# Four output products moved ahead of the last turn, two copies given to ScalarE, and some stages of head and end at other steps

## What is computed

```python
x = x + xattn(layernorm(x), ctx)     # 6 layers: self attention, cross attention over
                                     # 2048 context rows, feed-forward; all have a null key
x = x + attn(layernorm(x))           # one causal attention, 16 heads of 8
x = x + ffn(layernorm(x))            # a recurrent cell over the 4 elements:
#   f = sigmoid(x_t @ wf.T + c @ uf.T + bf); i = sigmoid(...); g = tanh(...)
#   c = f * c + i * g
#   out_t = tanh(x_t @ wo.T + c_final @ uo.T + bo)      for each element t
```

## Time and profile before

| | |
|---|---|
| median of 3 runs | 2582.73 us (2582.8, 2582.73, 2577.71) |
| the profiled execution | 2579.03 us |
| its span, first to last instruction | 2577.3 us |
| PE, DVE, ACT, POOL busy | 96%, 86%, 80%, 24% |
| granted TensorE clock, mean | 0.979 of full |
| head, before the heart of the first run | 0 to about 85 us |
| end, after the last heart | from about 2489 us |

### The profile page before, as it was taken

The page is one execution under the profiler, slowest core; times in us unless marked ns, Lnnn a source line. Parts: engine busy times, 40 slices in busy tenths (PEclk is TensorE's granted clock), DMA queues, the critical chain, the costliest instruction groups (busy, mean ns, idle before and its releaser), DMA issues.

```text
span 2577.3 us, 38071 instructions
## 1 busy us (share of the span) xinstructions
PE 2483.9 (96%) x12652; PEld 1532.9 (59%) x12652; DVE 2220.7 (86%) x4417; ACT 2053.5 (80%) x3977; POOL 615.2 (24%) x400
## 2 busy tenths in 40 slices
PE   4899999999999999999999999999999999999987
PEld 2456656656656656566566566566566566665566
DVE  6789889898898898898898898988988988989865
ACT  2788888888888888878888888888888888888743
POOL 3322312312313213123123123122132131231000
PEclk8899999999999999999999999999999999999986
DMA  3000010000001001001001001001001000000000
GB/s 130 25 9 17 26 36 17 25 11 37 26 14 39 15 11 47 9 17 53 9 17 47 9 17 53 9 17 47 3 23 36 17 25 30 17 9 26 1 1 5
DMA packets 16573, 63.56 MB, mean 25 GB/s; under 512 B 2241, under 2 KB 7410, under 8 KB 11642
## 3 DMA queue, kind: packets, MB, share of 16 engines
q1 hardware_dynamic: 16378, 61.13, 7.3%
HBM read 48.25 MB, written 0.29 MB: 19 GB/s over the span
## 4 chain that ended last, share of the span: by engine, by line
PE 71%; DVE 17%; ACT 5%; issue 4%; POOL 2%; DMA 0%; SPq 0%; DVEq 0%; POOLq 0%; ACTq 0%
PE psS L1108 20%; PE psO L1156 11%; PE psO L1157 11%; PE psO L1159 11%; DVE PL L690 5%; PE psL L1202 3%; ACT P L940 2%; PE psL L1213 2%; PE psL L1108 2%; PE psL L1220 2%; ACT PH L937 2%; DVE back_x L762 1%; DVE V L740 1%; POOL back_rstd L455 1%; PE psL L1101 1%
## 5 line engine op out<-in xcount | busy, mean ns | idle before, releaser
L937 ACT ACTIVATE PH<-psS 128x512 fp32r<-128x512 f32 x1536 | 1031.9, 672 | 180.7 <-PE psS L1108 160.9
L940 ACT ACTIVATE P<-psS 128x512 f32<-128x512 f32 x1536 | 1038.0, 676 | 109.8 <-DVE PL L690 109.7
L690 DVE TENSOR_TENSOR PL<-P,PH 128x512 fp32r<-128x512 f32 x1536 | 1040.5, 716 | 81.1 <-ACT P L940 71.3
L1108 PE MATMUL psS<-QT,KT 128*128 128x512 f16 x3072 | 923.6, 384 | 0.4 <-ACT P L940 0.3
L1156 PE MATMUL psO<-PH,V 128*128 128x512 f32 x1536 | 876.7, 571 | 0.0
L1157 PE MATMUL psO<-PH,VL 128*64 128x512 f32 x1536 | 607.1, 395 | 0.0
L1159 PE MATMUL psO<-PL,V 128*128 128x512 f32 x1536 | 606.0, 395 | 0.4 <-DVE PL L690 0.4
L1108 PEld LDWEIGHTS psS<-QT,KT 128*128 128x128 f16 x3072 | 218.1, 100 | 367.7 <-issue 282.4
L1156 PEld LDWEIGHTS psO<-PH,V 128*128 128x128 f32 x1536 | 292.4, 190 | 177.8 <-ACT PH L937 9.8
L1159 PEld LDWEIGHTS psO<-PL,V 128*128 128x128 f32 x1536 | 288.4, 188 | 152.4 <-DVE PL L690 0.9
L455 POOL TENSOR_TENSOR rn<-ssc,neghalf 128x16 f32<-128x16 f32 (+4 forms) x75 | 240.8, 3211 | 341.1 <-DVE ssc L624 264.1
(11 more groups left out here) (370 smaller groups left out, 2858.4 us busy)
## 6 DMA issues: line engine op xcount, KB each, us to landing
ctx_sb<-ctxT SPq DMA_DIRECT2D x24, 1024.0 KB, 4.7
KT<-KT SPq DMA_DIRECT2D x48, 256.0 KB, 3.7
W<-wpack SPq DMA_DIRECT2D x6, 1280.0 KB, 5.3
W<-wpack SPq DMA_DIRECT2D x6, 1088.0 KB, 7.4
W<-wpack SPq DMA_DIRECT2D x6, 576.0 KB, 5.7
KT<-biasM SPq DMA_DIRECT2D x1, 1024.0 KB
W<-tail_w SPq DMA_DIRECT2D x1, 832.0 KB
P<-biasW SPq DMA_DIRECT2D x1, 512.0 KB
```

What stands on the lines that cost most here:

```text
L690: nc_v.tensor_tensor(PL[:, here, :], P[:, t % PSLOTS, :], PH[:, here, :], ALU.subtract).then_inc(sem("p_lo"), 1)
L937: nc_a.activation(PH[:, t % HSLOTS, :], bank, ACT.Exp, scale=SIM_SCALE).then_inc(sem("p_hi"), 1)
L940: nc_a.activation(P[:, t % PSLOTS, :], bank, ACT.Exp, scale=SIM_SCALE).then_inc(sem("ca_exp"), 1)
L1108: ins = mm(bank, keys[part], q, start=(part == 0), stop=(part == 1))
```

## The change

The output products of each element become stages (`v_output0` to `v_output3`). Three stand ahead of `v_turn_z`, the fourth behind `v_gates3`. In setup, ScalarE makes the copy of the null values and scales them in place; VectorE waits for it and does the third operation. ScalarE has only that stage ahead of its first work of the head. One semaphore is folded into another, with the same order. The tables have some stages at other steps.

```diff
-            140: ["v_turn_z"],
-            141: ["v_gates3"],
+            140: ["v_output0", "v_output1", "v_output2", "v_turn_z"],
+            141: ["v_gates3", "v_output3"],
...
             def s_values():
-                setup(nc_v.tensor_copy(NVH[:], NV))
-                setup(nc_v.tensor_scalar(NV, NV, row_whole, None, ALU.mult))
+                dve.wait_ge(sem("values"), 1)
                 setup(nc_v.scalar_tensor_tensor(out=NVH[:], in0=NVH[:].bitcast(F32), scalar=row_high, in1=NV, op0=ALU.mult, op1=ALU.add))
...
+            def s_values():                              # ScalarE, first in its order
+                act.wait_ge(sem("consts_in"), 16 * 6)
+                nc_a.activation(NVH[:], NV, ACT.Copy)
+                nc_a.activation(NV, NV, ACT.Copy, scale=row_whole).then_inc(sem("values"), 1)
...
+                def output():
+                    pe.wait_ge(sem("z_T"), b + 1)
+                    mm(BANKS_OUT[b][:, 0:128], zT[:, b, :], tail_w(T_WO), start=True, stop=False)
+                    mm(BANKS_OUT[b][:, 0:128], ones[:], bo_row[:], start=False, stop=False)
...
-            for t in range(B):
-                mm(BANKS_OUT[t][:, 0:128], zT[:, t, :], tail_w(T_WO), start=True, stop=False)
-                mm(BANKS_OUT[t][:, 0:128], ones[:], bo_row[:], start=False, stop=False)
             pe.wait_ge(sem("c_ready"), B + 1)
```

More of the change, by code:

```diff
@@ L261, in build @@
             12: ["f_kv2", "h_kv2"], 13: ["f_kv3", "h_kv3"], 14: ["b_wo", "t0_turn_y2"],
-            18: ["f_turn_q_sa", "h_turn_q_sa", "b_turn", "t0_qkv"],
-            20: ["f_turn_k_sa", "h_turn_k_sa", "b_gate", "f_sn", "h_sn", "t1_turn_fin"], 21: ["t0_s0"],
+            18: ["f_turn_q_sa", "b_turn", "t0_qkv"], 19: ["h_turn_q_sa"],
+            20: ["f_turn_k_sa", "b_gate", "f_sn", "t1_turn_fin"], 21: ["h_turn_k_sa", "h_sn", "t0_s0"],
             22: ["f_sk0", "h_sk0", "t1_proj"], 23: ["f_sk1", "h_sk1", "t0_s1"], 25: ["f_sv0", "h_sv0", "t1_turn_y2"],
[4 rows of a table removed]
@@ L269, in build @@
[L269 to L272, removed]
[6 rows of a table removed]
[5 rows of a table added]
+            52: ["f_turn_ca", "h_turn_ca", "l_gate"], 53: ["t0_turn_z", "t1_pv1", "f_proj_ca", "h_proj_ca"],
@@ L279, in build @@
+            54: ["u_turn_fin"], 55: ["t1_pv2", "f_turn_k", "h_turn_k"], 56: ["u_proj"], 57: ["t1_pv3"], 58: ["l_up"],
+            59: ["t1_turn_o"], 60: ["t1_wo"], 61: ["h_turn_q_ca", "l_down"], 63: ["f_turn_q_ca", "t1_turn_z"],
+            64: ["b_down"], 68: ["u_turn_y2", "u_qkv"], 70: ["v_turn_fin"], 72: ["u_gates0"], 73: ["v_proj"], 75: ["u_s0"],
[6 rows of a table added]
         }
         PLAN_ACT = {
-            2: ["f_raw_sa", "h_raw_sa"], 3: ["f_raw_sa2", "h_raw_sa2"], 8: ["f_sq_sa", "h_sq_sa", "f_kraw0", "h_kraw0"],
@@ L282, in build @@
-            9: ["f_kraw1", "h_kraw1"], 10: ["s_table"], 12: ["h_hi_sa", "f_kraw2", "h_kraw2"], 13: ["f_hi_sa"],
-            15: ["f_kraw3", "h_kraw3"], 16: ["f_ksq", "h_ksq"], 17: ["f_QT_sa", "h_QT_sa"], 20: ["f_sne", "h_sne"],
[3 rows of a table removed]
-            47: ["t1_back2"], 53: ["f_raw_ca", "h_raw_ca", "f_sq_ca", "h_sq_ca"], 54: ["l_tanh"], 55: ["f_KT", "h_KT"],
-            57: ["h_hi_ca"], 59: ["f_hi_ca"], 61: ["h_QT_ca"], 63: ["f_QT_ca"], 72: ["u_gates0"], 87: ["u_exp0"],
-            88: ["u_exp1"], 92: ["u_exp2"], 95: ["v_exp0", "u_exp3"], 96: ["u_back0"], 97: ["u_back2"], 98: ["u_gates1"],
@@ L290, in build @@
-            102: ["v_exp1"], 103: ["v_exp2"], 106: ["v_exp3"], 107: ["v_back0"], 109: ["v_back2"], 130: ["v_gates2"],
-            147: ["v_gates3"],
+            0: ["s_values"], 2: ["f_raw_sa", "h_raw_sa"], 3: ["f_raw_sa2", "h_raw_sa2"],
+            8: ["f_sq_sa", "h_sq_sa", "f_kraw0", "h_kraw0"], 9: ["f_kraw1", "h_kraw1"], 10: ["s_table"],
+            12: ["h_hi_sa", "f_kraw2"], 13: ["f_hi_sa"], 15: ["f_kraw3", "h_kraw2", "h_kraw3"], 16: ["f_ksq"],
+            17: ["h_ksq", "f_QT_sa"], 18: ["h_QT_sa"], 20: ["f_sne"], 21: ["h_sne", "b_tanh", "t0_exp0"],
[3 rows of a table added]
@@ L318, in build @@
             65: ["u_gain", "v_largest"], 69: ["u_own"], 71: ["u_key0"], 72: ["u_key1", "v_final", "u_cell0"], 74: ["v_in"],
[1 row of a table removed]
[1 row of a table added]
             88: ["v_key0"], 90: ["v_key1", "u_mask2"], 91: ["v_mask0", "u_mask3"], 94: ["v_key2"], 95: ["u_back1"],
[1 row of a table removed]
-            108: ["u_cell1", "u_cols"], 110: ["v_back1"], 111: ["u_res", "v_back3", "v_sums"], 117: ["u_z"], 125: ["v_out"],
[1 row of a table added]
+            108: ["u_cols"], 110: ["v_back1"], 111: ["u_res", "u_cell1", "v_back3", "v_sums"], 117: ["u_z"], 125: ["v_out"],
             133: ["v_cols"], 134: ["v_cell2"], 135: ["v_res"], 141: ["v_z"], 147: ["v_cell3"],
@@ L329, in build @@
             36: ["f_ca", "h_ca", "s_row1", "l_out", "l_ff"], 41: ["f_ca_q", "h_ca_q"], 46: ["u_fin"],
-            49: ["f_low_ca", "h_low_ca"], 51: ["r_row2"], 52: ["r_row3"], 54: ["t0_z"], 56: ["u_y", "t1_z"], 60: ["u_y2"],
-            65: ["v_fin"], 74: ["v_y"], 79: ["v_y2"], 110: ["u_z"], 135: ["v_z"],
+            49: ["f_low_ca", "h_low_ca"], 51: ["r_row2"], 52: ["r_row3"], 54: ["t0_z"], 55: ["u_y"], 56: ["t1_z"],
+            60: ["u_y2"], 65: ["v_fin"], 74: ["v_y"], 79: ["v_y2"], 110: ["u_z"], 135: ["v_z"],
         }
@@ L570, in s_turned @@
             def s_turned():
-                dve.wait_ge(sem("null_T"), 1)
+                dve.wait_ge(sem("bias_mm"), 2)
                 nc_v.tensor_copy(NKC[:], null_turned[:, 0:2, 0:2 * L]).then_inc(sem("NKC"), 1)
@@ L596, in s_table @@
                 for g in range(4):
-                    dve.wait_ge(sem("bias_mm"), g + 2)
+                    dve.wait_ge(sem("bias_mm"), g + 3)
                     dve.wait_ge(sem("bias_moved"), 128)
@@ L1025, in _ @@
             stages = {
-                "s_table": s_table,
+                "s_table": s_table, "s_values": s_values,
                 "f_raw_sa": f_raw_sa, "f_raw_sa2": f_raw_sa2, "f_sq_sa": f_sq_sa, "f_hi_sa": halves("sa", 17), "f_QT_sa": queries("sa"),
@@ L1082, in s_null @@
                     ins = nc.tensor.transpose(null_turned[:, i, 0:2 * L], nks[:, i:i + 2].rearrange("p a d -> p (a d)"), ident16[0:2 * L, 0:2 * L])
-                ins.then_inc(sem("null_T"), 1)
+                ins.then_inc(sem("bias_mm"), 1)
             def s_table():
@@ L1375, in on @@
                 stages.update({base + "turn_fin": turn("fin"), base + "proj": proj, base + "turn_y2": turn("y2"), base + "qkv": qkv,
-                               base + "turn_o": turn_out, base + "wo": project_tail, base + "turn_z": turn("z"), f"{CELL[b]}_gates{b}": gates})
+                               base + "turn_o": turn_out, base + "wo": project_tail, base + "turn_z": turn("z"), f"{CELL[b]}_gates{b}": gates, f"v_output{b}": output})
                 for c in range(4):
```

5 lines of the change are left out of this document (3 added, 2 removed), and 46 rows, old and new, of tables (PLAN_ACT, PLAN_DVE, PLAN_PE).

## The result

The changed kernel takes 2566.99 us (median of 5 runs, 2564.04 to 2567.64) against 2581.53 for the kernel before (5 runs, 2577.71 to 2582.8): ratio 0.9943, 95% interval 0.9929 to 0.9956. The forecast was 2576.7 with a range from 2570.5 to 2581: right in its sign, wrong in its size, and the result lies outside the range. The profiled execution took 2564.04 us (span 2562.3, mean clock 0.984, where before had 0.979).

A forecast was written before the change was run, and what follows sets the result against it. The prediction saw a nearly full clock and TensorE busy for 96% of the span, with four avoidable waits. Gains of 0.8 + 1.15 + 2.4 + 1.7 = 6.05 us off the median gave 2576.7 us, range 2570.5 to 2581.

The forecast's parts named there:

- The head: Start to null scores: copy and scaling moved from VectorE into ScalarE's idle time gain 0.8 us, bounds 0 and 1.2.
- the third and fourth part of that wait for TensorE: Head: these bias table parts wait for flips ending at 31.17, so the queries' norm starts only 0.7 us earlier.
- The last feed-forward: VectorE takes the turned rows as soon as they are ready, gaining 1.15 us; bounds 0.5 and 1.3.
- Attention of u and v: Near the end: products moved into TensorE's idle 2.40 us gain 2.4 us; bounds 0.4 and 3.0, or 4.5.
- The 3.0 at full clock: Attention of u and v: at full clock v's last scores start at 2539.8 instead of 2542.77, 3.0 us earlier.
- rival B: Attention of u and v: the filled gap keeps TensorE's clock up longer, 2.5 us more gain, 2574.2 us; chance 0.14.
- the narrow products again: Argument against the clock staying up in the attention of u and v: value products are only 8 columns wide.
- The outputs: Kernel's end: three output pairs moved ahead of z's turn start the final products 1.7 us earlier; bounds 1.0 and 1.8.
- 0.1 to 0.5: Kernel's end: how many us late z would be if a stall came on one output pair.
- The last run's window: Window of the last run, where a few stages move: no gain, 0 us with 0.5 either way.
- nothing in the change touches what spreads them: Whole kernel: the runs' spread, 2577.71 to 2582.8 us, stays untouched, so the 6.05 us come off the median.

The follow-up runs named there:

- e4: Kernel before with only the output products made stages between the last turns: mean 2576.2 us over 11 runs, ratio 0.9989 to the kernel before.
- e5: The changed kernel run again with nothing changed: mean 2570.2 us over 6 runs, ratio 0.9969 to the kernel before.
- e9: The changed kernel run a third time with nothing changed: mean 2569.4 us over 10 runs, ratio 0.9973 to the kernel before.
- e1: Kernel before with only the head's edits (null values' copy and scaling on ScalarE, moved front stages): mean 2576.3 us over 11 runs, ratio 0.9990.
- e3: Kernel before with only the last feed-forward's moves (turned rows taken earlier, u's stages behind): mean 2576.5 us over 11 runs, ratio 0.9987.

## Why the prediction was wrong

Its sum of 6.05 us met a change of 10.2 ± 1.4 in the mean and 14.5 in the medians of the first five runs. The two first traces are 15.0 us apart. The four places that the sum names hold 7.9 of it: 2.4 in the head, 1.1 in the last feed-forward, 2.4 up to v's last scores, 2.1 behind v's projection. The other 7.1 lie where it had nothing: 3.5 behind v's last scores, 2.2 in the last run's window, 0.9 in and behind the last output projection, 0.5 ahead of v's projection. The 0.6 won in the head behind the null scores and the 0.6 lost in the 23 windows cancel. Step by step:

- **The head, 0.8 forecast, 2.4 measured: the term that was mis-sized.** The step that failed is "the third and fourth part of that wait for TensorE, whose flips end at 31.17". That the end of the flips and the start of the table's second half stood 0.14 us apart in the profile was a coincidence: other profiles of the old order (e4) have the flips done by 29.6 and null scores still at 40.68. What bound was VectorE's own row of work, four value copies (1.58 us) behind the sums. Second, GpSimd's pair took 1.92 us beside VectorE's instructions, and 1.18 when they came earlier or were gone. That the moves on ScalarE cost nothing was right: 0.84 and 0.92 us from 7.93 on, in the idle time. The Trainium skill's estimate ("ScalarE: Activation LUTs", "Rules for kernel authors", 0.94) lies just above both.
- **The last feed-forward, 1.15:** 1.06, right.
- **Attention of u and v, 2.4:** 2.4 between the two first traces and 2.9 in the mean of all profiles, but this hit is in part luck. The 3.0 at full clock was counted from 2542.77, a time that the old order reached with TensorE at a mean clock of 0.64 for the last 4.67 us. In e4 the old order has the full clock there and v's last scores 1.6 us sooner; at the same clock the new order brings them 1.2 earlier, and v's value products 0.7. What was priced as rival B, at 2.5 us and a chance of 0.14, came on top in every profile: 5.6 to 5.8 us behind the scores of v, where eight profiles without the moves have 8.1 in the mean, 2.3 more. Its opponent argument, "the narrow products again", did not hold for this stretch: the same narrow products ran through at full clock (2533.94 to 2539.51 above). It may hold for the next one, where the clock fell within v's narrow products.
- **The outputs, 1.7:** 1.75 of it is the wait that was named (2571.03 to 2572.78 before). The 2.1 of the first traces holds more time at full clock besides (a mean of 0.74 and not 0.63). What was left out is a pair at half clock, 1.45 us and not 0.85: z late by "0.1 to 0.5" is 1.4 in the executions that have the half clock there, and the old order loses 3.7 behind the cell (12.6 against 10.3 in sum).
- **The last run's window, 0:** right. The 2.15 us between the two first traces is a clock that differs in executions of one and the same program: e5 and e9 have 106.1 there where after had 103.9.
- **The step that failed for the range** is "nothing in the change touches what spreads them". What spreads the runs is TensorE's time at half clock. The mean of it fell from 109 to 93 us, at 0.26 us each worth some 4 us; the first five runs lay 2.7 us lower again. The base did its part too: 6.05 was taken off a median of three runs, 2582.73, where the mean of 84 is 2579.0 and the profiled execution stood at 2579.03.

Taken to the same time at half clock by the fitted line, the changed kernel is some 6 us below before (10.2 less 16 times 0.26; the expectation of e9 had 5.8). That is the forecast's 6.05, by other terms: 2.4 for the head, 1.1, 0.7 for the order in the attention and 1.7 for the outputs. The head was 1.6 too small and the attention 1.7 too large, and that they cancel is luck. The fitted slope and the one profile e4 carry this sum, so it is an estimate.

The missing 4 us are the half clock that fell. Most of that lies where the moves of u and v work: behind 2535 us the profiles with them have 12.5 to 25.4 us at half clock (18.4 in the mean of ten), those without 29.1 to 36.2, and 14.4 in e4 (30.9 in the mean of eight). Why the moves keep the clock up (the gap or the narrow products) stays open, as said above. That e1, e3 and e4 lower the mean too (by 2 to 5 us, with intervals of 3 to 7) was not settled.

## What to carry to other kernels

Two times that stand together in one profile do not show which waits for which; take the engine's own queue away first, and look at the sum of work behind the wait. When a move is priced at full clock, price the old order at full clock too; a time read at half clock makes the move look better than it is. Where TensorE waits near the ends of a kernel, moves that fill a wait can be worth its length and also the clock of what comes behind it, so give such a rival its price in the range. And know the spread of both kernels before a difference of a half per cent is explained: two traces of one and the same program differ in the clock by 2 us in one window.

## What the runs showed of the hardware

- Granted half clock moves between executions of one program: the same window took 103.9 or 106.1 us, the same head 44.4 to 47.4 from null scores to core, and in a line over all runs each microsecond at half clock goes with 0.26 us of time.
- Products that nobody reads, in waits of 2.8 to 5.0 us, cut the time at half clock from 93 to 67 us and the kernel by 4.1 ± 1.7 us. The Trainium skill ("TensorE: Matmul & The Clock Gate", "Part 1: The HAM clock gate") has activity release the throttle, and the number of slow products at a kernel's start differ from run to run; the fall from 93 to 67 us agrees with the first. But a busy TensorE did not always have the full clock: in the kernel before it was busy for all of 15.83 us at a clock of 0.50. Of the second the traces show that the changed kernel had 34.1 us at half clock in its head in one profile and 47.8 in two (after; e5, e9), and that the last 180 us differ too.
- Behind a gap of 2.42 us in TensorE the clock stayed at 1.00 for 12.4 us in e4 (up to 2553.7). In the kernel before, behind the same gap of 2.42, it fell to 0.50 after 1.3 us (at 2539.4).
- A pair of GpSimd operations of 128x128 took 1.92 us beside VectorE's scalar_tensor_tensor of 768 columns (20.60 to 21.62), and 1.18 in after, where that ran from 19.30 to 20.30. All six profiles with VectorE's copies have 1.91 or 1.92, the other twelve 1.18 to 1.20. The row of before, from its timeline:
```profile
20.66 1.92 POOL L493 TENSOR_TENSOR qsq<-qraw,C 128x128 f32<-128x128 f32 x2 [2.18 <-ACT qraw L960]
```
The Trainium skill ("GPSIMD Engine Reference", "1. Specifications") names contention with VectorE's instructions that have two SBUF inputs; the row of before agrees (that instruction reads NVH and P), and the pair has 0.74 us as its price.
